# A graph layer with a residual and a layer norm on one core: runs of four rows for x, four unsplit chunks instead of six, ScalarE's normalise, and a new warm-up

## The chip, the cores and the metric

The kernel runs on one core of a Trainium2 chip. The metric is the device time of one execution in microseconds. The profile shows one execution, whose span is a little shorter than its device time.

## The reference

The inputs are x (4096 x 256, fp32) and an adjacency matrix adj (4096 x 4096, fp32, sparse, all entries at or above zero).

```python
mask = adj > 0
head = mask / max(sqrt(sum(mask * mask, axis=-1)), 1e-12)   # 1/sqrt(neighbours)
inc = adj + head
edge = (inc @ x) / sum(inc, axis=-1)
out = layernorm(x + edge, axis=-1)                          # eps 1e-5, no affine
```

The kernel works with inc scaled by the row's norm: the square root of the neighbour count times adj, plus the mask. The scale cancels between the product and the degree.

## The kernel before

**Layout.** A tile is 128 rows of adj; there are 32 tiles (`TILES`). A tile lies in SBUF as four quarters of [128 partitions x 1024]: quarter q holds rows 32q to 32q+31 of the tile, and partition block g (32 partitions) holds their columns 1024g to 1024g+1023. So a 32x32 block transpose of a quarter gives, for each of 32 chunks b, 128 values of the contraction dimension on the partitions. x is laid out the same way: partition 32g+j holds row 1024g+32b+j of x for chunk b.

**Per tile.** `sign_quarter` (L226, ScalarE) counts the positive entries of a quarter with an accumulated Sign. TensorE adds the partial sums of the four partition blocks with `quad_sum` (L650; in the warm-up L629, one matmul for each quarter). VectorE makes the count (`count_of` L453, `count_early` L447), GpSimd raises it to the power 0.5 (`norm_of` L360, `norm_early` L390). `scale_quarter` (L237, ScalarE) writes norm times adj to PSUM, `inc_quarter` (L465, VectorE) adds the mask, `transpose_quarter` (L481, VectorE) transposes into `incT`.

**The product.** fp32 matmuls run as two instructions for one chunk ("unsplit" or native, L655). To avoid them, 26 of the 32 chunks (`SPLIT`) are split in two parts of the type fp32r: `inc` into hi (rounded by ScalarE L248 for the quarters in `ACT_HI`, by GpSimd L385 for those in `POOL_HI`) and lo (the difference, GpSimd L380), x into hi (ScalarE L253) and lo (VectorE L441). A split chunk costs TensorE one matmul hi times (x hi, x lo) of 512 columns (L699) and one matmul lo times x hi of 256 columns (L708). The other six chunks (`NATIVE`) stay unsplit. Tiles 0 and 1 are unsplit altogether, for the split of x isn't there yet. Every tile accumulates in one of two PSUM tensors `edge`.

**The residual.** VectorE divides by the degree and adds x (L508, L512), takes statistics (L516, L521), GpSimd takes the power -0.5 (`rstd_of` L364), VectorE normalises (L533), SP stores.

**Order.** Every engine's instructions are written out by hand: VectorE works on tile t while TensorE is at tile t-1; `residual(t-2)` is threaded through VectorE's tile t and `normalise(t-3)` with it. ScalarE's `tile(t)` holds two scales of t, two signs of t+1, two signs of t+2, two scales of t+1 and two hi quarters of t. Raw tiles are double buffered: tile t+2's quarter k is loaded once `inc_quarter(t, k)` is done. SP issues all loads and stores in one queue; `store(t-4)` stands behind the loads of tile t. `sum_quadrants(t)` stands at position hi 3 of TensorE's tile t (`SUMS_AT`); it needs the signs of tile t+2, and `count_of(t+2)` on VectorE needs it. In the warm-up, tiles 0 to 3 (`EARLY`) have sums, counts and norms of their own for each quarter, so that a quarter can be scaled before the others have come.

## Time and profile before

| what | value |
|---|---|
| median of 3 runs | 427.29 us (424.83 to 427.61) |
| the profiled execution | 428.19 us, its span 426.4 us |
| busy share of the span | PE 93%, DVE 87%, ACT 81%, POOL 81% |
| chain that ended last | L699 35%, L708 18%, L655 15% (all PE) |
| mean granted clock of TensorE | 0.996 of full speed |
| HBM traffic | 79.7 MB, 187 GB/s over the span |

The chain is followed back from the last instruction. PE is the matmul engine, DVE is VectorE, ACT ScalarE, POOL GpSimd, SP the engine that issues DMAs. A mean duration counts from start to end, and two instructions that follow each other overlap a little; where that matters, start to start is read from a timeline.

### The profile page before, as it was taken

The page shows a single profiled execution, that of the slowest core. Times are in us where ns is not written, and L with a number is a line of the kernel's source. Part 1 is how long each engine was busy: PE and PEld are TensorE (multiplying, and loading weights), DVE is VectorE, ACT ScalarE, POOL GpSimd, SP SyncE. Part 2 cuts the span into 40 slices and gives each one's busy share as a digit, 9 for nine tenths or more (in the row PEclk, how much of TensorE's full clock was granted, in tenths as well). Part 3 has the DMA queues.
Part 4 walks back from the last instruction along what each step waited for, and adds up shares of the span by engine and source line. Part 5 has one row for each costly group of instructions (what it writes and reads, how often), then busy time and mean ns, then how long its engine had stood idle before and what let it go on. Part 6 is the DMA issues. An engine that isn't in the chain of part 4 may idle for free.

```text
span 426.4 us, 8925 instructions
## 1 busy us (share of the span) xinstructions
PE 396.4 (93%) x2174; PEld 349.5 (82%) x2174; DVE 370.9 (87%) x750; ACT 343.3 (81%) x450; POOL 344.2 (81%) x273
## 2 busy tenths in 40 slices
PE   1299987989999999999999999999999999999995
PEld 0277866868888888888888888888888888888884
DVE  0986776899999999999999999999999999999942
ACT  4874968989998888888989889898988988886300
POOL 3110386799999999999999999999999999999960
PEclk9999998999999999999999999999999999999999
DMA  8999986666766666666666666776666676670010
GB/s 231 258 233 244 261 220 182 173 190 200 215 188 197 194 203 216 213 196 192 200 184 200 186 200 202 221 212 190 200 186 199 186 199 194 206 221 25 26 38 12
DMA packets 38220, 79.86 MB, mean 187 GB/s; under 512 B 9536, under 2 KB 21824, under 8 KB 38208
## 3 DMA queue, kind: packets, MB, share of 16 engines
q1 hardware_dynamic: 37824, 78.68, 64.8%
q10 hardware_dynamic: 384, 1.05, 0.9%
q8 instruction: 4, 0.07, 0.1%
q14 instruction: 8, 0.07, 0.1%
HBM read 75.50 MB, written 4.19 MB: 187 GB/s over the span
## 4 chain that ended last, share of the span: by engine, by line
PE 70%; issue 3%; POOL 2%; DVE 2%; ACT 0%; POOLq 0%; DVEq 0%
PE edge L699 35%; PE edge L708 18%; PE edge L655 15%; POOL inc_split L380 2%; DVE inc L465 1%; PE sums L650 1%; DVE incT L481 1%; POOL inc_split L385 0%; ACT scaled L237 0%; POOLq L45 0%; POOL rstd L364 0%; DVE rows L533 0%; DVE rows L508 0%; DVE rows L512 0%; DVE stats L516 0%
## 5 line engine op out<-in xcount | busy, mean ns | idle before, releaser
L380 POOL TENSOR_TENSOR inc_split<-incT,inc_split 128x832 fp32r<-128x832 f32 x120 | 236.9, 1985 | 8.9 <-DVE incT L481 6.1
L699 PE MATMUL edge<-x_split,inc_split 128*128 128x512 f32 (+1 forms) x810 | 195.4, 392 | 0.0
L226 ACT ACTIVATE sign_out<-raw,sign_bias 128x1024 bf16<-128x1024 f32 x128 | 146.3, 1143 | 32.0 <-DMA raw<-in_adj_dram 30.5
L699 PEld LDWEIGHTS edge<-x_split,inc_split 128*128 128x128 f32 x810 | 145.9, 188 | 26.7
L465 DVE SCALAR_TENSOR_TENSOR inc<-raw,scaled 128x1024 f32<-128x1024 f32 x128 | 153.5, 1199 | 4.1 <-ACT scaled L237 4.1
L481 DVE STREAM_TRANSPOSE incT<-inc 128x1024 f32<-128x1024 f32 x128 | 155.8, 1227 | 0.2
L237 ACT ACTIVATE scaled<-raw,norm 128x1024 f32<-128x1024 f32 x128 | 141.7, 1107 | 13.2 <-POOL norm L390 6.6
L708 PEld LDWEIGHTS edge<-x_split,inc_split 128*128 128x128 f32 x780 | 99.1, 194 | 2.3
L708 PE MATMUL edge<-x_split,inc_split 128*128 128x256 f32 x780 | 100.0, 286 | 0.0
L655 PE MATMUL edge<-x_native,incT 128*128 128x256 f32 x384 | 92.2, 389 | 1.1 <-DVE count L447 0.7
L655 PEld LDWEIGHTS edge<-x_native,incT 128*128 128x128 f32 x384 | 71.9, 194 | 10.1 <-DVE incT L481 0.8
L248 ACT CAST inc_split<-incT 128x832 fp32r<-128x832 f32 x60 | 52.6, 876 | 9.8 <-DVE incT L481 8.0
L385 POOL TENSOR_SCALAR inc_split<-incT 128x832 fp32r<-128x832 f32 x60 | 55.1, 919 | 0.0
L390 POOL TENSOR_TENSOR norm<-count,half 128x1 f32<-128x1 f32 x16 | 8.9, 555 | 42.7 <-DVE count L447 42.7
L360 POOL TENSOR_TENSOR norm<-count,half 128x4 f32<-128x4 f32 x28 | 28.7, 1025 | 15.5 <-DVE count L453 15.5
L364 POOL TENSOR_TENSOR rstd<-var_eps,minus_half 128x1 f32<-128x1 f32 x32 | 17.9, 560 | 11.0 <-DVE var_eps L524 11.0
L655 PE MATMUL edge<-x_stage,incT 128*128 128x256 f32 x104 | 24.6, 386 | 0.8 <-DMA x_stage<-in_x_dram 0.8
L226 ACT ACTIVATION_READ_ACCUMULATOR sign_out<-raw,sign_bias 128x1 f32 x128 | 23.9, 187 | 0.0
L655 PEld LDWEIGHTS edge<-x_stage,incT 128*128 128x128 f32 x104 | 19.1, 190 | 4.3 <-DMA x_stage<-in_x_dram 2.0
L533 DVE TENSOR_SCALAR rows<-rows,mean_var,rstd 128x256 f32<-128x256 f32 x32 | 20.9, 655 | 1.6 <-POOL rstd L364 1.6
L508 DVE SCALAR_TENSOR_TENSOR rows<-edge,rdeg,rows 128x256 f32<-128x256 f32 x30 | 13.2, 439 | 10.2 <-PE edge L708 10.2
L453 DVE TENSOR_SCALAR count<-sums 128x4 f32<-128x4 f32 x28 | 4.5, 162 | 18.2 <-PE sums L650 18.2
(35 smaller groups left out, 119.5 us busy)
## 6 DMA issues: line engine op xcount, KB each, us to landing
raw<-in_adj_dram SPq DMA_DIRECT2D x504, 128.0 KB, 2.6
rows<-in_x_dram SPq DMA_DIRECT2D x32, 128.0 KB, 2.1
out_dram<-rows SPq DMA_DIRECT2D x32, 128.0 KB, 1.7
x_stage<-in_x_dram SPq DMA_DIRECT2D x8, 224.0 KB, 10.3
x_stage<-in_x_dram SPq DMA_DIRECT2D x8, 192.0 KB, 9.8
raw<-in_adj_dram ACTq DMA_DIRECT2D x8, 128.0 KB, 5.4
x_native<-in_x_dram SPq DMA_DIRECT2D x4, 192.0 KB, 7.3
```

Of the source, the lines that this page charges most:

```text
L226: nc.scalar.activation(sign_out[:, :], raw[:, s, q, :], ACT.Sign, scale=SIGN_SCALE, bias=sign_bias[:, 0:1], accum_out=part_sums[:, s, 1, q ...
L237: nc.scalar.mul(scaled[q % 2][:, :], raw[:, s, q, :], norm[:, s, q:q + 1]).then_inc(scaled_ready, 1)
L248: nc.scalar.copy(hi_of(s, q), incT[:, s, 0:SPLIT, q, :]).then_inc(hi_by_act, 1)
L360: nc.gpsimd.tensor_tensor(norm[:, s, :], count[:, s, :], half[:, :], ALU.pow).then_inc(norm_ready, 1)
L380: nc.gpsimd.tensor_tensor(lo_of(s, q), incT[:, s, 0:SPLIT, q, :], hi_of(s, q).bitcast(fp32), ALU.subtract).then_inc(lo_by_pool, 1)
L385: nc.gpsimd.tensor_scalar(hi_of(s, q), incT[:, s, 0:SPLIT, q, :], 1.0, 1.0, ALU.mult, ALU.mult).then_inc(hi_by_pool, 1)
L465: nc.vector.scalar_tensor_tensor(inc[:, q, :], raw[:, s, q, :], 0.0, scaled[q % 2][:, :], ALU.is_gt, ALU.add, accum_out=part_sums[:, s, 0, ...
L481: nc.vector.transpose(incT[:, s, :, q, :], inc[:, q, :].rearrange("p (b j) -> p b j", j=SQ)).then_inc(incT_ready, 1)
L533: nc.vector.tensor_scalar(result[:, s, :], y[:, s, :], mean_var[:, s, 0:1], rstd[:, s:s + 1], ALU.subtract, ALU.mult).then_inc(result_read ...
L655: return nc.tensor.matmul(edge[s][:, 0:D], incT[:, s, b, :, :].rearrange("p q j -> p (q j)"), x_of_b, start=start, stop=stop)
L699: last = nc.tensor.matmul(edge[s][:, c0:c1], inc_split[s][:, 0, b, :, :].rearrange("p q j -> p (q j)"), x_split[:, b, :, :].rearrange("p h ...
L708: last = nc.tensor.matmul(edge[s][:, D:2 * D], inc_split[s][:, 1, b, :, :].rearrange("p q j -> p (q j)"), x_split[:, b, 0, :], start=False ...
```

## The change

- x is laid out with four consecutive rows on one partition: partition 32g+j holds rows 128b'+4j+l of the block g for the chunks 4b'+l. A DMA run is then 4 KB (four rows) where it was 1 KB. To match, `transpose_quarter` reads inc with a stride of four elements (16 bytes) in place of unit stride.
- `NATIVE` goes from 6 to 4, so `SPLIT` from 26 to 28.
- ScalarE rounds three quarters of hi and GpSimd one (two and two before).
- The normalise moves from VectorE to ScalarE (Identity with scale rstd and bias shift); VectorE computes shift = -mean * rstd. The store stands one tile later in SP's queue.
- Sign writes int8 into two alternating buffers, with an immediate bias in place of one read from SBUF.
- `EARLY` goes from 4 to 6; the orders of the warm-up are rewritten on every engine, the last tiles are written out, and `SUMS_AT` goes from hi 3 to hi 12.

The core of the diff; ScalarE's, GpSimd's and VectorE's warm-up and tail are lists of calls in the same manner as the loops shown:

```diff
-    NATIVE = 6
+    NATIVE = 4
     SPLIT = B - NATIVE
     EPS = 1e-5
     SIGN_SCALE = 2.0 ** 60
     SIGN_BIAS = -2.0 ** -90
     FOUR_DMAS = 16 * G
+    EARLY = 6
     PORT_ORDER = [0, 2, 1, 3]
     adj_v = adj.rearrange("(t q r) (g c) -> t g r q c", q=G, r=SQ, g=G)
-    x_v = x.rearrange("(g b j) d -> g j b d", g=G, j=SQ)
+    x_v = x.rearrange("(g b j l) d -> g j b (l d)", g=G, j=SQ, l=4)
...
-        sign_out = sb("sign_out", [P, COLS], bf16)
+        sign_out = sb("sign_out", [P, 2, COLS], mybir.dt.int8)
...
+        shift = sb("shift", [P, 2], fp32)
...
+        early_sums = [[sums[0], sums[1], edge[0], edge[1]], [sums[0], sums[1], edge[1], sums[0]]]
+        early_sums += [[sums[1 - t % 2]] * G for t in range(2, EARLY)]
+        early_read = [[0, 0, 0, 0], [1, 2, 4, 5]] + [[8] + [G * t + q for q in range(1, G)] for t in range(2, EARLY)]
...
-        X_AT = [0, 7, 14, 20, SPLIT]
+        X_AT = [0, 8, 16, 24, SPLIT]
         X_PIECES = len(X_AT) - 1
-        EARLY = 4
-        ACT_HI = [0, 3]
-        POOL_HI = [1, 2]
+        ACT_HI = [0, 2, 3]
+        POOL_HI = [1]
...
+            def load_x(c):
+                for g in PORT_ORDER:
+                    sp.dma_start(x_stage[SQ * g:SQ * (g + 1), X_AT[c]:X_AT[c + 1], :].rearrange("p (b l) d -> p b (l d)", l=4),
+                                 x_v[g, :, X_AT[c] // 4:X_AT[c + 1] // 4, :]).then_inc(x_in[c], 16)
+            def load_x_native():
+                for g in PORT_ORDER:
+                    sp.dma_start(x_native[SQ * g:SQ * (g + 1), :, :].rearrange("p (b l) d -> p b (l d)", l=4),
+                                 x_v[g, :, SPLIT // 4:B // 4, :]).then_inc(x_native_in, 16)
             for k in range(G):
                 for g in (0, 1):
                     load_piece(sp, 0, 0, k, g)
-            for g in PORT_ORDER:
-                sp.dma_start(x_native[SQ * g:SQ * (g + 1), :, :], x_v[g, :, SPLIT:B, :]).then_inc(x_native_in, 16)
+            load_x_native()
             for k in range(G):
                 load_quarter(1, 1, k, False)
-            for c in range(4):
-                for g in PORT_ORDER:
-                    sp.dma_start(x_stage[SQ * g:SQ * (g + 1), X_AT[c]:X_AT[c + 1], :],
-                                 x_v[g, :, X_AT[c]:X_AT[c + 1], :]).then_inc(x_in[c], 16)
-            for s in range(2):
-                load_residual(s, s, False)
-            for s in range(2):
+            load_x(0)
+            load_x(1)
+            load_x(2)
+            load_x(3)
+            load_residual(0, 0, False)
+            for k in range(G):
+                load_quarter(2, 0, k, True)
+            load_residual(1, 1, False)
+            for k in range(G):
+                load_quarter(3, 1, k, True)
+            for t in range(4, 6):
                 for k in range(G):
-                    load_quarter(2 + s, s, k, True)
-            with sp.Fori(2, PAIRS) as u:
+                    load_quarter(t, t % 2, k, True)
+                if t == 5:
+                    store(0, 0)
+                load_residual(t - 2, t % 2, True)
+            with sp.Fori(3, PAIRS) as u:
...
-                    store(t - 4, s)
+                    store(t - 5, 1 - s)
...
-                    act.wait_ge(signs_ready, G * t + q)
+                    act.wait_ge(signs_ready, G * t + q - 1)
                 if early_reuse:
                     act.wait_ge(early_summed, G * (t - 2) + q + 1)
                 elif q == 0 and reuse:
                     act.wait_ge(summed, t - 3)
-                nc.scalar.activation(sign_out[:, :], raw[:, s, q, :], ACT.Sign, scale=SIGN_SCALE,
-                                     bias=sign_bias[:, 0:1], accum_out=part_sums[:, s, 1, q:q + 1]).then_inc(signs_ready, 1)
+                nc.scalar.activation(sign_out[:, q % 2, :], raw[:, s, q, :], ACT.Sign, scale=SIGN_SCALE,
+                                     bias=SIGN_BIAS, accum_out=part_sums[:, s, 1, q:q + 1]).then_inc(signs_ready, 1)
...
+            def normalise(t, s, u, reuse=True):
+                act.wait_ge(shift_ready, t + 1)
+                if reuse:
+                    act.wait_ge(stored[s], 16 * u)
+                nc.scalar.activation(result[:, s, :], y[:, s, :], ACT.Identity, scale=rstd[:, s:s + 1],
+                                     bias=shift[:, s:s + 1]).then_inc(result_ready, 1)
...
             sign_early(0, 0)
+            scale_early(0, 0)
             sign_early(0, 1)
-            scale_early(0, 0)
+            scale_early(0, 1)
             sign_early(0, 2)
-            scale_early(0, 1)
             sign_early(0, 3)
+            sign_early(1, 0)
             scale_early(0, 2)
             scale_early(0, 3)
-            sign_early(1, 0)
             sign_early(1, 1)
+            sign_early(1, 2)
             scale_early(1, 0)
-            sign_early(1, 2)
             scale_early(1, 1)
+            scale_early(1, 2)
             sign_early(1, 3)
-            scale_early(1, 2)
+            split_x_hi(0)
+            split_x_hi(1)
             scale_early(1, 3)
-            for c in range(X_PIECES):
-                split_x_hi(c)
+            split_x_hi(2)
+            split_x_hi(3)
...
+            with act.Fori(3, PAIRS - 2) as u:
+                scale_quarter(2 * u, 0, 2)
+                sign_quarter(2 * u + 1, 1, u, 2)
+                sign_quarter(2 * u + 1, 1, u, 3)
+                round_quarter(2 * u, 0, 0)
+                scale_quarter(2 * u, 0, 3)
+                normalise(2 * u - 3, 1, u - 2)
+                sign_quarter(2 * u + 2, 0, u + 1, 0)
+                scale_quarter(2 * u + 1, 1, 0)
+                sign_quarter(2 * u + 2, 0, u + 1, 1)
+                scale_quarter(2 * u + 1, 1, 1)
+                round_quarter(2 * u, 0, 2)
+                round_quarter(2 * u, 0, 3)
...
+            with pool.Fori(3, PAIRS - 2) as u:
+                norm_of(2 * u + 1, 1)
+                low_quarter(2 * u, 0, 0, behind=1)
+                round_quarter(2 * u, 0, 1, own=False)
+                rstd_of(2 * u - 2, 0)
+                low_quarter(2 * u, 0, 1)
+                low_quarter(2 * u, 0, 2)
+                low_quarter(2 * u, 0, 3)
...
-                nc.vector.transpose(incT[:, s, :, q, :],
-                                    inc[:, q, :].rearrange("p (b j) -> p b j", j=SQ)).then_inc(incT_ready, 1)
-            def residual(t, s, u, native=False):
-                def step(ins):
-                    ins.then_inc(dve_step, 1)
-                def after(k):
-                    dve.wait_ge(dve_step, steps_to(t) + k - (1 if native and k > 2 else 0))
+                nc.vector.transpose(incT[:, s, :, q, :].rearrange("p (b l) j -> p b l j", l=4),
+                                    inc[:, q, :].rearrange("p (b j l) -> p b l j", j=SQ, l=4)).then_inc(incT_ready, 1)
...
+            def shift_of(t, s):
                 dve.wait_ge(rstd_ready, t + 1)
+                nc.vector.scalar_tensor_tensor(shift[:, s:s + 1], mean_var[:, s, 0:1], -1.0, rstd[:, s:s + 1],
+                                               ALU.mult, ALU.mult).then_inc(shift_ready, 1)
...
+            with dve.Fori(3, PAIRS - 2) as u:
+                inc_quarter(2 * u, 0, 0)
+                degree(2 * u - 2, 0)
+                shift_of(2 * u - 3, 1)
+                inc_quarter(2 * u, 0, 1)
+                inverse_degree(2 * u - 2, 0)
+                transpose_quarter(2 * u, 0, 0)
+                y_first(2 * u - 2, 0, u - 1)
+                inc_quarter(2 * u, 0, 2)
+                y_second(2 * u - 2, 0)
+                count_of(2 * u + 1, 1)
+                transpose_quarter(2 * u, 0, 1)
+                statistics(2 * u - 2, 0)
+                inc_quarter(2 * u, 0, 3)
+                mean_variance(2 * u - 2, 0)
+                transpose_quarter(2 * u, 0, 2)
+                variance_eps(2 * u - 2, 0)
+                transpose_quarter(2 * u, 0, 3)
...
-                if t == 3 and q == 0:
-                    pe.wait_ge(dve_step, steps_to(0) + 1)
+                if t >= 3 and q == 0:
+                    pe.wait_ge(dve_step, steps_to(t - 3) + 1)
...
-            SUMS_AT = ("hi", 3)
...
+            sum_early(1, 2)
+            unsplit_chunks(0, 0, 0, B, {9: lambda: sum_early(1, 3), 18: lambda: sum_degree(0, 0)})
+            unsplit_chunks(1, 1, 0, B, {3: lambda: sum_early(2, 0), 7: lambda: sum_early(2, 1),
+                                        13: lambda: sum_early(2, 2), 16: lambda: sum_early(2, 3),
+                                        20: lambda: sum_degree(1, 1), 22: lambda: sum_early(3, 0),
+                                        31: lambda: sum_early(3, 1)})
+            tile(2, 0, {("native", 3): lambda: sum_early(3, 2), ("hi", 9): lambda: sum_early(3, 3),
+                        ("lo", 0): lambda: sum_early(4, 0), ("lo", 9): lambda: sum_degree(2, 0),
+                        ("lo", 10): lambda: sum_early(4, 1)}, first=True)
+            tile(3, 1, {("native", 2): lambda: sum_early(4, 2), ("hi", 8): lambda: sum_early(4, 3),
+                        ("hi", 10): lambda: sum_early(5, 0), ("hi", 18): lambda: sum_early(5, 1),
+                        ("hi", 22): lambda: sum_degree(3, 1)})
+            tile(4, 0, {("native", 0): lambda: sum_early(5, 2), ("native", 3): lambda: sum_early(5, 3),
+                        ("hi", 25): lambda: sum_quadrants(4, 0, early=True)})
+            tile(5, 1, {("hi", 18): lambda: sum_quadrants(5, 1, early=True)})
+            SUMS_AT = ("hi", 12)
+            with pe.Fori(3, PAIRS - 1) as u:
```

## Rows read from the trace of the kernel before

**Rows 1.** Chain that ended last, in order of time: start us, us, what.

```profile
207.55 2.59 PE edge L655 x12
210.14 0.71 PE edge L699 x4
...
210.97 5.33 PE edge L699 x23
216.30 3.11 PE edge L708 x26
219.42 2.59 PE edge L655 x12
```

**Rows 2.** Busy time of each engine in one tile: PE, PEld, DVE, ACT, POOL, clock, DMA.

```profile
210.14:222.01 11.87, 11.87 (x70) 10.56 (x69) 11.22 (x24) 10.63 (x15) 11.14 (x9) 1.00 0.65 195
```

**Rows 3.** Groups of instructions by form: busy us, mean ns, idle before, releaser.

```profile
L380 POOL TENSOR_TENSOR inc_split<-incT,inc_split 128x832 fp32r<-128x832 f32 x120 | 236.9, 1985 | 8.9 <-DVE incT L481 6.1 <-issue 0.2
...
L481 DVE STREAM_TRANSPOSE incT<-inc 128x1024 f32<-128x1024 f32 x128 | 155.8, 1227 | 0.2
...
L226 ACT ACTIVATE sign_out<-raw,sign_bias 128x1024 bf16<-128x1024 f32 x128 | 146.3, 1143 | 32.0 <-DMA raw<-in_adj_dram 30.5
...
L237 ACT ACTIVATE scaled<-raw,norm 128x1024 f32<-128x1024 f32 x128 | 141.7, 1107 | 13.2 <-POOL norm L390 6.6 <-DVE inc L465 3.6 <-POOL norm L360 2.4
...
L385 POOL TENSOR_SCALAR inc_split<-incT 128x832 fp32r<-128x832 f32 x60 | 55.1, 919 | 0.0
L248 ACT CAST inc_split<-incT 128x832 fp32r<-128x832 f32 x60 | 52.6, 876 | 9.8 <-DVE incT L481 8.0 <-PE edge L699 1.4
...
L533 DVE TENSOR_SCALAR rows<-rows,mean_var,rstd 128x256 f32<-128x256 f32 x32 | 20.9, 655 | 1.6 <-POOL rstd L364 1.6
...
L253 ACT CAST x_split<-x_stage 128x1792 fp32r<-128x1792 f32 x2 | 3.3, 1674 | 0.0
```

**Rows 4.** Timeline of ScalarE within one tile: start us, us, instruction.

```profile
212.80 1.10 ACT L237 ACTIVATE scaled<-raw,norm 128x1024 f32<-128x1024 f32 x1
213.84 1.13 ACT L226 ACTIVATE sign_out<-raw,sign_bias 128x1024 bf16<-128x1024 f32 x1
...
214.97 1.10 ACT L237 ACTIVATE scaled<-raw,norm 128x1024 f32<-128x1024 f32 x1
...
220.86 0.87 ACT L248 CAST inc_split<-incT 128x832 fp32r<-128x832 f32 x1
221.63 1.11 ACT L237 ACTIVATE scaled<-raw,norm 128x1024 f32<-128x1024 f32 x1
223.79 1.15 ACT L226 ACTIVATE sign_out<-raw,sign_bias 128x1024 bf16<-128x1024 f32 x1 [1.04 <-DMA raw<-in_adj_dram]
```

**Rows 5.** Timeline of VectorE: the count that waits for TensorE.

```profile
211.01 0.16 DVE L453 TENSOR_SCALAR count<-sums 128x4 f32<-128x4 f32 x1 [0.65 <-PE sums L650]
```

**Rows 6.** Timeline of TensorE in the first fifth of the span.

```profile
21.13 1.22 PE L655 MATMUL edge<-x_native,incT 128*128 128x256 f32 x2 [0.71 <-DVE count L447]
...
37.19 2.86 PE L655 MATMUL edge<-x_stage,incT 128*128 128x256 f32 x12 [0.66 <-DMA x_stage<-in_x_dram]
...
70.70 0.36 PE L650 MATMUL sums<-part_sums,quad_sum 128*128 128x8 f32 x2 [2.52 <-DVE incT L481]
...
100.56 2.75 PE L655 MATMUL edge<-x_native,incT 128*128 128x256 f32 x12
```

**Rows 7.** Timeline of ScalarE: the first sign of tile 2.

```profile
40.46 1.15 ACT L226 ACTIVATE sign_out<-raw,sign_bias 128x1024 bf16<-128x1024 f32 x1 [1.81 <-DMA raw<-in_adj_dram]
```

**Rows 8.** Three stretches of 2 us, columns as in Rows 2.

```profile
28.00:30.00 2.00, 2.00 (x11) 1.60 (x9) 1.97 (x4) 2.00 (x2) 0.00 (x0) 1.00 1.13 233
50.00:52.00 2.00, 2.00 (x12) 1.78 (x11) 1.41 (x3) 2.00 (x4) 1.17 (x2) 1.00 1.04 262
72.00:74.00 2.00, 2.00 (x11) 2.00 (x11) 0.35 (x1) 1.59 (x2) 2.00 (x3) 0.50 0.05 14
```

**Rows 9.** Timeline of VectorE: the last instruction of the last tile.

```profile
423.78 0.41 DVE L533 TENSOR_SCALAR rows<-rows,mean_var,rstd 128x256 f32<-128x256 f32 x1 [0.66 <-POOL rstd L364]
```

More of the change, by code:

```diff
@@ L314, in _ @@
             sign_early(3, 1)
+            normalise(0, 0, 0, reuse=False)
+            round_quarter(2, 0, 2, reuse=False)
             sign_early(3, 2)
@@ new lines, in _ @@
+            round_quarter(3, 1, 2, staged=True)
+            scale_early(4, 0)
+            round_quarter(3, 1, 3, staged=True)
+            sign_early(5, 0)
+            sign_early(5, 1)
+            scale_early(4, 1)
+            scale_early(4, 2)
+            normalise(1, 1, 0, reuse=False)
+            sign_early(5, 2)
+            sign_early(5, 3)
+            round_quarter(4, 0, 0)
+            scale_early(4, 3)
+            sign_early(6, 0)
+            scale_early(5, 0)
+            round_quarter(4, 0, 2)
@@ new lines, in _ @@
+            scale_quarter(28, 0, 2)
+            sign_quarter(29, 1, 14, 2)
+            sign_quarter(29, 1, 14, 3)
+            round_quarter(28, 0, 0)
+            scale_quarter(28, 0, 3)
+            normalise(25, 1, 12)
+            sign_quarter(30, 0, 15, 0)
+            scale_quarter(29, 1, 0)
+            sign_quarter(30, 0, 15, 1)
+            scale_quarter(29, 1, 1)
+            round_quarter(28, 0, 2)
+            round_quarter(28, 0, 3)
+            scale_quarter(29, 1, 2)
+            sign_quarter(30, 0, 15, 2)
@@ new lines, in _ @@
+            sign_quarter(30, 0, 15, 3)
+            round_quarter(29, 1, 0)
+            scale_quarter(29, 1, 3)
+            normalise(26, 0, 13)
+            sign_quarter(31, 1, 15, 0)
+            scale_quarter(30, 0, 0)
+            sign_quarter(31, 1, 15, 1)
+            scale_quarter(30, 0, 1)
+            round_quarter(29, 1, 2)
+            round_quarter(29, 1, 3)
+            scale_quarter(30, 0, 2)
+            sign_quarter(31, 1, 15, 2)
+            sign_quarter(31, 1, 15, 3)
+            round_quarter(30, 0, 0)
@@ new lines, in _ @@
+            scale_quarter(30, 0, 3)
+            normalise(27, 1, 13)
+            scale_quarter(31, 1, 0)
+            scale_quarter(31, 1, 1)
+            round_quarter(30, 0, 2)
+            round_quarter(30, 0, 3)
+            scale_quarter(31, 1, 2)
+            round_quarter(31, 1, 0)
+            scale_quarter(31, 1, 3)
+            normalise(28, 0, 14)
+            round_quarter(31, 1, 2)
+            round_quarter(31, 1, 3)
+            normalise(29, 1, 14)
+            normalise(30, 0, 15)
@@ L339, in _ @@
+            normalise(31, 1, 15)
         @block.gpsimd
@@ L391, in norm_early @@
                                         ALU.pow).then_inc(early_norm, 1)
-            def tile(t, s, more=True):
-                if more:
-                    norm_of(t + 1, 1 - s)
-                low_quarter(t, s, 0, True, behind=1)
-                round_quarter(t, s, 1)
-                rstd_of(t - 2, s)
-                low_quarter(t, s, 1, behind=2)
-                round_quarter(t, s, 2)
-                low_quarter(t, s, 2)
-                low_quarter(t, s, 3)
-            for t in range(3):
-                for q in range(G):
-                    norm_early(t, q)
@@ L431, in _ @@
-            tile(TILES - 2, 0)
-            tile(TILES - 1, 1, more=False)
-            for s in range(2):
-                rstd_of(TILES - 2 + s, s)
+            norm_early(5, 0)
+            rstd_of(2, 0)
+            low_quarter(4, 0, 0)
+            round_quarter(4, 0, 1)
+            norm_early(5, 1)
+            norm_early(5, 2)
+            low_quarter(4, 0, 1)
+            low_quarter(4, 0, 2)
+            norm_early(5, 3)
+            low_quarter(4, 0, 3)
+            round_quarter(5, 1, 1)
@@ L611, in _ @@
-            tile(TILES - 2, 0, PAIRS - 1)
-            tile(TILES - 1, 1, PAIRS - 1, more=False)
-            normalise(TILES - 3, 1, PAIRS - 2, True)
-            for s in range(2):
-                for _ in residual(TILES - 2 + s, s, PAIRS - 1):
-                    pass
-                normalise(TILES - 2 + s, s, PAIRS - 1, True)
+            transpose_quarter(1, 1, 1, slot_split=False, reuse_slot=False)
+            split_x_lo(0)
+            inc_quarter(1, 1, 2, reuse_deg=False)
+            split_x_lo(1)
```

540 lines of the change are left out of this document (360 added, 180 removed).

## Prediction

> **What bounds the kernel now.** I read the chain that ended last first. From about 92 us on it is TensorE alone, tile after tile, with the same four pieces and no gap: 2.59 for twelve unsplit matmuls, 0.71 and 5.33 for hi, 3.11 for lo, 0.12 for the sums, and the next tile begins 11.87 us after the last [rows 1]. The window over one tile says the same from the other side: PE busy 11.87 of 11.87, VectorE 11.22, GpSimd 11.14, ScalarE 10.63 [rows 2]. So in the steady part only TensorE's own work counts, as long as no other engine needs more than TensorE does. ScalarE's slack shows as a wait for a raw load (1.04, [rows 4]), VectorE's as the wait for the sums (0.65, [rows 5]): both are waits of engines that are early.
>
> The first part is different. TensorE begins the product at 21.13 and tile 5 at 100.56 [rows 6]. At full speed two unsplit tiles (27.7) and three split ones (35.6) would take 63.3, so 16.1 us are lost there, to x that comes late (0.66 and shorter waits, at 37.19), and to sums that wait (2.52 at 70.70) [rows 6]. Behind that wait the granted clock was 0.50 in 72 to 74 us, which is 1.2 GHz, after TensorE had stood still from 68.2 to 70.7 [rows 8].
>
> **The steady part of the change.** An unsplit chunk costs 2 x 2.59/12 = 0.432, a split one 5.33/23 + 3.11/26 = 0.232 + 0.120 = 0.351 [rows 1]. Two chunks a tile change sides: -0.16, so 11.70 a tile if TensorE stays the bound. For the 27 tiles 5 to 31 that is 4.35 us. Whether it stays the bound is arithmetic on three queues, start to start:
>
> ScalarE. A scale takes 1.04, a sign with its accumulator read 1.13, a cast 0.77 [rows 4]: 4.16 + 4.52 + 1.54 = 10.2 now. A cast grows by (1674 - 876)/960 = 0.83 ns an element [rows 3], so 64 more make 0.82, three of them 2.47. A cast of 1024 would be 1036 ns by that slope where the sign is 1143; the sign reads its bias from SBUF, the cast nothing. So a sign without that read is 1.03, four 4.1. The normalise of 256 elements: 876 - 576 x 0.83 = 400, and two operands read from SBUF at 0.1 each, 0.6 long and 0.5 start to start. Sum 4.1 + 4.16 + 2.47 + 0.5 = 11.2, with 0.5 left under 11.70. If the sign stays at 1.13 it is 11.6. The Trainium skill, "ScalarE: Activation LUTs", section "What ACT_TABLE_LOAD costs", gives 93 ns for each pointer operand; the rows' 107 agree, and with 93 the sum would be 11.3. The alternating sign buffer takes away a wait of some 0.1 between two signs in a row, and the load that ScalarE waits for now stands behind a store that waits for the normalise; the store moves a tile later, so SP isn't held by it. I count these at nothing: they refill slack that the sum uses up.
>
> GpSimd. One round less, -0.92; four lows of 896 in place of 832, 4 x 1.985 x 64/832 = +0.61 and +0.07 for the round that stays [rows 3]: 11.14 - 0.24 = 10.9.
>
> VectorE. The normalise goes (0.65 [rows 3], some 0.6 start to start) and a one-column instruction comes (0.1): 11.22 becomes 10.7, plus whatever the stride costs in four transposes. 1.0 is left under 11.70: **0.25 for each transpose is free, all above it is paid 4 times a tile.** No row shows a read with a stride of 16 bytes. From below the bound is 0: nothing of the pattern can make the read shorter than the one in order. From above I take a second pass over the 1024 elements, at the slope of the casts 0.85, at worst 1.05. I take 0, for the nearest row is the transpose itself: 1227 ns for 1024 elements [rows 3], one plain pass with one operand read, although its output already jumps after every 32 elements. Against it speaks a rule. The Trainium skill, "SBUF — State Buffer", in its note on SBUF cachelines, says that each access to a new 16-byte line pays a penalty and that two hits on a line are needed for full speed, yet names four fp32 elements as a free stride in the same note; every access here goes to a new line. By its strict reading the transposes stretch (the third case below), by its loose one they don't; no run here shows which.
>
> The order. The sums move from hi 3 to hi 12, to 1.73 + 12 x 0.232 + 0.12 = 4.6 after a tile's start. VectorE has then to do the count, three transposes, one inc and small steps, 5.3, so its last transpose ends near 10.1 of 11.7; the last hi quarter is cast by ScalarE at about 11.2, and needed at 11.7 + 1.73. ScalarE's two signs that the sums need are done near 2.8 of the tile, before 4.6 (and would be late for hi 3 at 2.4: the move has a reason). GpSimd's fourth low ends near 4.3 of the next tile, lo begins at 8.3. Every wait on this way has over a microsecond in hand, so TensorE has no gap.
>
> **The warm-up.** Behind x everything is bound by the transfers: the DMA engines are full (share over 1.0) both at 28 us, where x comes in runs of 1 KB at 233 GB/s, and at 50 us, where adj comes in runs of 4 KB at 262 [rows 8]. x is 4.19 MB, 18.0 us against 16.0: all behind it comes 2.0 us sooner, with the second residual after tile 2 another 0.4. Step by step:
> Tile 0: its last transpose now stands behind the count of sign (1, 1), and I work out a start at 22.7, 1.5 later than 21.13 [rows 6]. That is hidden: the last piece of x lands near 35.3 (37.19 less 1.9), four chunks (1.73) are left after it, and by its own work tile 0 ends at 22.7 + 13.8 + 0.4 = 36.9. Tile 1 starts at 37.2.
> Tile 1: 13.8 of product, seven sums of 0.12. The first sign of tile 2 was at 40.46 behind a load [rows 7], now 38.1; its sum stands at chunk 3 (38.6) and waits 0.7, the fourth one, loads 2 us apart, about 0.5. Tile 2 starts at 53.2, and VectorE has its last transpose at 52.7.
> Tiles 2 to 4: 11.7 each, with five, four and three early sums (some 0.5 a tile) and up to 0.5 for hi quarters or sums that come just in time. I get 65.9, 78.7 and 90.9 for the starts of tiles 3, 4 and 5. No wait over 1 us is left in this walk, so no drop of the clock either. Against 100.56 [rows 6] that is 9.7 us. The bounds: all steps on time, and PE alone from 37.2, gives 37.2 + 14.7 + 3 x 12.1 = 88.2, 12.4; half of the gain lost to steps that miss by a microsecond, 95.7, 4.9.
>
> **The tail.** After the last product VectorE's 0.41 [rows 9] is replaced by the shift (0.15), a hop (0.2) and ScalarE's 0.6: +0.5.
>
> **Sum.** -4.35 - 9.7 + 0.5 = -13.55. Against the profiled 428.19 this is 414.6, against the median, 0.9 lower, 413.7. I say 414.
>
> **Rivals.**
> 1. ScalarE becomes the bound. Its 11.2 to 11.6 leaves 0.1 to 0.5, and it has waits on VectorE of 0.2 now. For it: a third cast waits for the last transpose of a tile. Against it: those waits lie where it is early. At 11.9 a tile in place of 11.70 it costs 27 x 0.2 = 5.4: 419 to 420. By the same size the half-lost warm-up gives 418.5.
> 2. The start isn't won: if the walk of tiles 0 to 4 misses as now, only -4.35 + 0.5 remains, 423.5. For it: 16 us are lost now in steps that the walk prices at 6, and ScalarE and VectorE run nearly full there. Against it: two causes of the loss, the runs of 1 KB and the sums of a whole tile for tile 4, are gone.
> 3. The other side: the strided transposes are slow. With D more for each, VectorE needs 10.7 + 4D a tile, and it decides from D = 0.25 on. With D = 0.6 (half of a second pass) 13.1 a tile, 27 x 1.4 = 38 over the forecast, 452; with D = 1.05 a tile is 14.9, 27 x 3.2 = 86, with 10 more in the warm-up, 510. For it: nothing in the trace excludes it. Against it: the jumps of its output cost nothing that shows in its 1227 ns. In the mild case (D below 0.25) only the warm-up feels it, by 1 to 2.
>
> **Chances.** Forecast, within 410 to 418: 0.60. Rival 1 or half the warm-up, 418 to 421.5: 0.17. Rival 2: 0.06. Rival 3: 0.14. Better than 410: 0.03. The range that leaves out no more than 2 in 10 reaches from 409.5 to 424, past rivals 1 and 2, short of rival 3. One per cent, 4.3 us, is about what a measurement can tell: faster (below 423) 0.82, within 0.04, slower 0.14.
>
> **What would show it.** L481's mean first of all: 1227 right, above 1480 rival 3. Then the tile in the chain: 11.70, with 1.73 for unsplit; ScalarE below 11.4 a tile and no wait of PE for a cast (rival 1); a sign at 1.04 and not 1.14; windows at 28 us with 260 GB/s; the start of tile 5 near 91; PEclk without a drop near 72. I'd be wrong above all by a stride that costs, then by early steps that meet late.

## The result and the profile after

The changed kernel takes 532.21 us (median of 4 runs, 531.63 to 534.89), the kernel before 427.45 beside it: 1.246 times as long (95% interval 1.240 to 1.252). I had said 414, so the forecast is wrong in its sign. The profiled execution took 531.63 with a span of 529.8.

The head of the page of the changed kernel, and its section on the chain that ended last:

```profile
span 529.8 us, 8912 instructions
...
PE 424.4 (80%) x2190; PEld 365.3 (69%) x2190; DVE 498.0 (94%) x756; ACT 378.0 (71%) x512; POOL 336.8 (64%) x248
...
issue 45%; DVE 44%; PE 4%; DVEq 2%; ACT 2%; POOL 2%; ACTq 1%; POOLq 0%
```

VectorE is busy 94% of the span and TensorE has 4% of the chain, where it had all of it in the steady part before [rows 1]. The "issue" entries of the chain lie inside VectorE's long instructions (the profile shows no releaser there). VectorE itself has hardly a gap: from 110.51 to 510.56 us, the starts of tiles 5 and 31 on TensorE, it is busy 399.42 of 400.05. One tile of the changed kernel, columns as in [rows 2]:

```profile
249.06:264.43 15.37, 12.00 (x67) 10.38 (x67) 15.37 (x25) 11.72 (x16) 10.78 (x8) 1.00 0.52 154
```

15.37 of 15.37 on VectorE, against 11.87 a tile before [rows 2]. From the start of tile 5 to the end of the last product it is 413.7 us where it was 320.6, which is 93.1 of the 103.4 by which the span grew (27 times 3.50 would be 94.5). Tile 5 begins at 110.51 and not at 100.56 [rows 6], which is another 10.0. The groups by form of the changed kernel, in the order of their busy time:

```profile
L629 DVE STREAM_TRANSPOSE incT<-inc 128x1024 f32<-128x1024 f32 x128 | 257.3, 2023 | 0.3
...
L613 DVE SCALAR_TENSOR_TENSOR inc<-raw,scaled 128x1024 f32<-128x1024 f32 x128 | 153.9, 1203 | 0.0
...
L234 ACT ACTIVATE sign_out<-raw 128x1024 int8<-128x1024 f32 x128 | 133.4, 1042 | 0.0
...
L256 ACT CAST inc_split<-incT 128x896 fp32r<-128x896 f32 x90 | 84.6, 940 | 105.6 <-DVE incT L629 105.5
...
L685 DVE SCALAR_TENSOR_TENSOR shift<-mean_var,rstd 128x1 f32<-128x1 f32 x32 | 49.5, 1548 | 0.7 <-POOL rstd L452 0.7
...
L268 ACT ACTIVATE rows<-rows,shift,rstd 128x256 f32<-128x256 f32 x32 | 18.8, 588 | 14.8 <-DVE shift L685 14.8
```

Two groups are out of line. The transpose takes 2023 ns where it took 1227 [rows 3]. And the shift, one column wide, takes 1548 ns; I had put 0.1 us for it. The other groups are as priced.

What the shift does in its 1.5 us is seen by laying two timelines of the changed kernel side by side. VectorE, at the start of the tile above:

```profile
250.25 1.72 DVE L685 SCALAR_TENSOR_TENSOR shift<-mean_var,rstd 128x1 f32<-128x1 f32 x1
251.90 1.21 DVE L613 SCALAR_TENSOR_TENSOR inc<-raw,scaled 128x1024 f32<-128x1024 f32 x1
```

GpSimd at the same time:

```profile
247.80 6.24 POOL L468 TENSOR_TENSOR inc_split<-incT,inc_split 128x896 fp32r<-128x896 f32 x3
```

Three subtractions of 2.08 us follow each other, so the second ends at 251.96. The shift, begun at 250.25, ends at 251.97: it ends with the GpSimd instruction that was in flight. Its shortest case in this trace is 155 ns, its median 1728. And it is a rule of this trace: 29 of the 32 shifts begin while a subtraction is under way, and all 29 end 0.01 to 0.02 after it. The other three begin with GpSimd idle and take 0.16.

### The profile page after: what moved, and what is told of

It reads as the page before. It is cut to its first block, busy times and chain, and to the rows that moved or that the text cites. A ratio compares the mean times of both kernels' runs of the same rounds, so it can differ in the third digit from the quotient of the medians.

```text
span 529.8 us, 8912 instructions
## 1 busy us (share of the span) xinstructions
PE 424.4 (80%) x2190; PEld 365.3 (69%) x2190; DVE 498.0 (94%) x756; ACT 378.0 (71%) x512; POOL 336.8 (64%) x248
## 4 chain that ended last, share of the span: by engine, by line
issue 45%; DVE 44%; PE 4%; DVEq 2%; ACT 2%; POOL 2%; ACTq 1%; POOLq 0%
DVE inc L613 22%; DVE incT L629 11%; PE edge L951 3%; DVE rows L661 2%; DVE stats L671 2%; DVE rows L666 2%; DVE shift L685 1%; POOL inc_split L468 1%; PE edge L996 1%; ACT sign_out L234 1%; DVE x_split L589 1%; ACTq L153 1%; DVE var_eps L680 1%; DVEq L612 1%; DVE mean_var L676 1%
## 5 line engine op out<-in xcount | busy, mean ns | idle before, releaser
L468 POOL TENSOR_TENSOR inc_split<-incT,inc_split 128x896 fp32r<-128x896 f32 x120 | 251.0, 2114 | 24.9 <-DVE incT L629 22.5
L629 DVE STREAM_TRANSPOSE incT<-inc 128x1024 f32<-128x1024 f32 x128 | 257.3, 2023 | 0.3
L996 PE MATMUL edge<-x_split,inc_split 128*128 128x512 f32 (+1 forms) x870 | 218.7, 404 | 0.0
L996 PEld LDWEIGHTS edge<-x_split,inc_split 128*128 128x128 f32 x870 | 164.3, 198 | 32.1
L256 ACT CAST inc_split<-incT 128x896 fp32r<-128x896 f32 x90 | 84.6, 940 | 105.6 <-DVE incT L629 105.5
L234 ACT ACTIVATE sign_out<-raw 128x1024 int8<-128x1024 f32 x128 | 133.4, 1042 | 0.0
L1005 PEld LDWEIGHTS edge<-x_split,inc_split 128*128 128x128 f32 x840 | 104.8, 191 | 2.3
L685 DVE SCALAR_TENSOR_TENSOR shift<-mean_var,rstd 128x1 f32<-128x1 f32 x32 | 49.5, 1548 | 0.7 <-POOL rstd L452 0.7
L482 POOL TENSOR_SCALAR inc_split<-incT 128x896 fp32r<-128x896 f32 x30 | 28.3, 944 | 2.8 <-DVE incT L629 2.8
L268 ACT ACTIVATE rows<-rows,shift,rstd 128x256 f32<-128x256 f32 x32 | 18.8, 588 | 14.8 <-DVE shift L685 14.8
L234 ACT ACTIVATION_READ_ACCUMULATOR sign_out<-raw 128x1 f32 x128 | 23.9, 187 | 0.0
```

What stands on the lines that cost most here:

```text
L234: nc.scalar.activation(sign_out[:, q % 2, :], raw[:, s, q, :], ACT.Sign, scale=SIGN_SCALE, bias=SIGN_BIAS, accum_out=part_sums[:, s, 1, q: ...
L256: nc.scalar.copy(hi_of(s, q), incT[:, s, 0:SPLIT, q, :]).then_inc(hi_by_act, 1)
L468: nc.gpsimd.tensor_tensor(lo_of(s, q), incT[:, s, 0:SPLIT, q, :], hi_of(s, q).bitcast(fp32), ALU.subtract).then_inc(lo_by_pool, 1)
L482: nc.gpsimd.tensor_scalar(hi_of(s, q), incT[:, s, 0:SPLIT, q, :], 1.0, 1.0, ALU.mult, ALU.mult).then_inc(hi_by_pool, 1)
L629: nc.vector.transpose(incT[:, s, :, q, :].rearrange("p (b l) j -> p b l j", l=4), inc[:, q, :].rearrange("p (b j l) -> p b l j", j=SQ, l=4 ...
L685: nc.vector.scalar_tensor_tensor(shift[:, s:s + 1], mean_var[:, s, 0:1], -1.0, rstd[:, s:s + 1], ALU.mult, ALU.mult).then_inc(shift_ready, 1)
```

## The experiments

**e1: the disputed costs by themselves.** A small program with the instructions alone. The transposes and the inc-like instruction are written once for each access pattern; then a shift in two forms and the transposes run beside a row of GpSimd's subtractions. The forms of the transpose and of the shift:

```
transpose(low in order, inc.rearrange("p (b j l) -> p b l j", j=32, l=1, 2, 4 or 8))
scalar_tensor_tensor(shift, mean, -1.0, rstd, mult, mult)     # two operands of SBUF
tensor_scalar(shift, mean, rstd, -1.0, mult, mult)            # one, and rstd as its scalar
```

> The disputed prices by themselves, nothing of the reference is computed. Theory: the stride of 16 bytes costs the transpose 0.8 us with no other engine at work (about 2.0 against 1.2 for 1024 elements), and the one-column instruction with two SBUF operands takes 0.1 to 0.2 us alone, but up to 2.1 beside GpSimd's subtractions, for it waits until the one in flight ends; the form with one SBUF operand and a pointer scalar stays at 0.1 to 0.2. Rival on the stride: the slow transposes come from sharing SBUF with GpSimd, then stride 4 alone takes 1.2. Where the price begins is open: stride 2 (8 bytes) and stride 8 (32 bytes) tell. Rival on the shift: it is slow by itself, then it takes 1.5 alone too.

Groups by form of the probe:

```profile
L95 DVE STREAM_TRANSPOSE low<-inc 128x1024 f32<-128x1024 f32 x6 | 12.0, 2006 | 0.2
L93 DVE STREAM_TRANSPOSE low<-inc 128x1024 f32<-128x1024 f32 x6 | 11.9, 1982 | 0.2
L99 DVE SCALAR_TENSOR_TENSOR low<-raw,scaled 128x1024 f32<-128x1024 f32 x6 | 11.7, 1958 | 0.2
L104 DVE SCALAR_TENSOR_TENSOR low<-raw,scaled 128x1024 f32<-128x1024 f32 x6 | 11.7, 1957 | 0.2
L114 DVE STREAM_TRANSPOSE low<-inc 128x1024 f32<-128x1024 f32 x4 | 8.1, 2013 | 0.1
L70 ACT ACTIVATE scaled<-raw 128x1024 f32<-128x1024 f32 x4 | 7.9, 1964 | 0.1
L89 DVE STREAM_TRANSPOSE low<-inc 128x1024 f32<-128x1024 f32 x6 | 7.5, 1246 | 20.5 <-ACT rstd L74 20.4
L91 DVE STREAM_TRANSPOSE low<-inc 128x1024 f32<-128x1024 f32 x6 | 7.5, 1246 | 0.2
L97 DVE SCALAR_TENSOR_TENSOR low<-raw,scaled 128x1024 f32<-128x1024 f32 x6 | 7.3, 1221 | 0.2
...
L68 ACT ACTIVATE scaled<-raw 128x1024 f32<-128x1024 f32 x4 | 4.1, 1027 | 0.1
L111 DVE SCALAR_TENSOR_TENSOR shift<-mean,rstd 128x1 f32<-128x1 f32 x4 | 3.5, 862 | 0.1
...
L112 DVE TENSOR_SCALAR shift<-mean,rstd 128x1 f32<-128x1 f32 x4 | 0.9, 214 | 0.1
```

L89, L91, L93 and L95 read with strides of 1, 2, 4 and 8 elements: 1246, 1246, 1982, 2006 ns. It is a step between 8 and 16 bytes and not a slope; from 16 bytes to 32 it hardly grows. It isn't the transpose's own either: the two-operand instruction goes from 1221 (L97) to 1958 with a strided read (L99) and to 1957 with a strided write alone (L104), and ScalarE from 1027 (L68) to 1964 (L70) with a strided read. The difference on 1024 elements is 0.74 to 0.76 us on VectorE, six tenths of the instruction's time again, and 0.94 on ScalarE, nine tenths of it. The transpose is hardly slower beside GpSimd (L114, 2013), so GpSimd is not what makes it 2023 in the changed kernel. The two-operand shift has 862 in the mean in the part beside GpSimd and 159 alone; the one-operand form 214 both ways. The 862 is no price either: two of the four took 0.15 and 0.16 (one began before GpSimd did, one at the very start of a subtraction), the other two 1.47 and 1.67. Both theories of the expectation came.

One of the two long shifts of L111, all engines of the probe:

```profile
95.72 5.22 POOL L121 TENSOR_TENSOR half<-raw 128x896 f32<-128x896 f32 x3
...
99.48 1.47 DVE L111 SCALAR_TENSOR_TENSOR shift<-mean,rstd 128x1 f32<-128x1 f32 x1
```

95.72 + 5.22 = 100.94 is the end of the third subtraction, 99.48 + 1.47 = 100.95 that of the shift.

**e2: the kernel before, with the stride alone.**

```diff
-                nc.vector.transpose(incT[:, s, :, q, :],
-                                    inc[:, q, :].rearrange("p (b j) -> p b j", j=SQ)).then_inc(incT_ready, 1)
+                nc.vector.transpose(incT[:, s, :, q, :].rearrange("p (b l) j -> p b l j", l=4),
+                                    inc[:, q, :].rearrange("p (b j l) -> p b l j", j=SQ, l=4)).then_inc(incT_ready, 1)
```

> The kernel before with strided reads in the transposes and nothing else; x stays in its old layout, so the product pairs rows of x wrongly. Theory: each transpose 2.0 us, VectorE 11.2 + 3.2 = 14.4 a tile, it becomes the bound, 27 x 2.6 = 70 and some 8 more in the warm-up: 505 us. Rival (the stride is slow only together with the rest of the change): 427 to 435 us.

498.53 us, 1.167 (1.164 to 1.169). A stretch of it, which is a little longer than a tile:

```profile
200.00:214.42 14.42, 12.41 (x69) 10.58 (x68) 14.42 (x24) 10.99 (x15) 11.10 (x8) 1.00 0.58 172
```

VectorE never stands still: from tile 5's start (109.32) to tile 31's (478.81) it is busy 369.49 of 369.49 us. That is 14.2 a tile; by VectorE's 11.22 of before [rows 2] and four times 0.80 it would be 14.4. Of the 0.2 between them 0.1 is the normalise, which takes 546 ns in the mean here and took 655 before [rows 3]. This one edit, of two lines, costs 71 us: 61 of them lie behind tile 5's start, 9 in the warm-up. The 505 of the expectation was 6 too high, as it took 14.4 for the tile.

**e3: the changed kernel without the stride.** The diff of e2 the other way round, in the changed kernel.

> The changed kernel with transposes that read in order; x stays in the new layout, so rows of x are paired wrongly. Theory: VectorE falls from 15.37 to 12.2 a tile and is still the bound through the shift, which stays near 1.5 us; 27 x 3.2 = 86 and some 10 in the warm-up come back: 436 us, above the kernel before. Rival (the wait of the shift is an accident of the phase and goes with the stride): 11.7 a tile, 415 to 420 us.

419.05 us, 0.980 (0.978 to 0.982). The rival in its expectation was right. One tile of e3:

```profile
218.88:230.58 11.70, 11.70 (x69) 10.40 (x68) 11.38 (x24) 11.60 (x17) 10.79 (x8) 1.00 0.65 201
```

The shift's group by form in e3:

```profile
L685 DVE SCALAR_TENSOR_TENSOR shift<-mean_var,rstd 128x1 f32<-128x1 f32 x32 | 27.8, 868 | 0.7 <-POOL rstd L452 0.7
```

TensorE is the bound again, at the 11.70 of the prediction. The shift still waits, 0.87 in the mean, yet VectorE has room for it: in most tiles it begins 1.34 into a subtraction and has 0.8 left to wait.

One case is out of line. The traced execution took 425.39 us, and in it stand, on VectorE, GpSimd and TensorE:

```profile
95.24 5.51 DVE L685 SCALAR_TENSOR_TENSOR shift<-mean_var,rstd 128x1 f32<-128x1 f32 x1
...
94.46 6.27 POOL L468 TENSOR_TENSOR inc_split<-incT,inc_split 128x896 fp32r<-128x896 f32 x3
...
110.28 3.78 PE L951 MATMUL edge<-x_native,incT 128*128 128x256 f32 x8 [4.22 <-DVE incT L629]
```

This shift begins during the first of three subtractions in a row and ends, at 100.75, with the third (94.46 + 6.27 = 100.73). It let two go by where the others waited for one at most. The transposes behind it come late, TensorE stands still for 4.22 and then has a granted clock of 0.50 (1.2 GHz) up to 113.50, and two tiles take 16.08 and 14.73. Two of the six executions of e3 took 424.14 and 425.39, the other four 418.01 to 419.38; of the 42 of e4 and of e6 to e12, which have the other form of the shift, none took more than 419.58. So in e3 the wait is worth nothing in most executions, and 7 us in this one. Whether the 424.14 had the same cause was not traced.

**e4: e3 with the shift in the form of one operand.**

```diff
-                nc.vector.scalar_tensor_tensor(shift[:, s:s + 1], mean_var[:, s, 0:1], -1.0, rstd[:, s:s + 1],
-                                               ALU.mult, ALU.mult).then_inc(shift_ready, 1)
+                nc.vector.tensor_scalar(shift[:, s:s + 1], mean_var[:, s, 0:1], rstd[:, s:s + 1], -1.0,
+                                        ALU.mult, ALU.mult).then_inc(shift_ready, 1)
```

> As e3, and the shift made by an instruction with one SBUF operand and a pointer scalar, which should not wait for GpSimd. Theory, and the walk of the prediction: VectorE 10.7 a tile, TensorE the bound at 11.70, tile 5 at 91 us, 414 us. Rivals: ScalarE bounds at 11.9 (420 us); the warm-up is not won (423 us); the shift still waits (as e3).

418.49 us, 0.979 (0.976 to 0.981), no different from e3's median. One tile of e4:

```profile
212.42:224.12 11.70, 11.70 (x69) 10.40 (x68) 10.78 (x24) 11.53 (x17) 10.78 (x8) 1.00 0.66 200
```

The shift's group by form in e4:

```profile
L685 DVE TENSOR_SCALAR shift<-mean_var,rstd 128x1 f32<-128x1 f32 x32 | 6.6, 207 | 0.7 <-POOL rstd L452 0.7
```

VectorE falls from 11.38 to 10.78 and the tile doesn't move.

**e5: the changed kernel, stride and all, with e4's shift.**

> The changed kernel, strides kept, with the shift made from one SBUF operand and a pointer scalar. Theory: in the changed kernel the shift waits 1.5 us a tile for a subtraction of GpSimd, and VectorE is the bound, so all of it is paid: 15.37 - 1.5 = 13.85 a tile, 27 x 1.5 = 41 and a few more in the warm-up, 488 us. Rival (as in e3, where the same edit was worth nothing: the time moves into another wait): 525 to 532 us.

493.09 us, 1.153 (1.150 to 1.156), where I had expected 488. One tile of it:

```profile
248.86:262.75 13.89, 12.05 (x67) 10.38 (x67) 13.89 (x24) 11.72 (x16) 10.77 (x8) 1.00 0.56 169
```

The tiles are not all alike here: most lie between 13.8 and 14.3, and 14.04 is their mean. So the same edit that is worth nothing in e3's median is worth 532.2 - 493.1 = 39.1 us here. From tile 5's start to the last product's end it takes 376.9 us, the changed kernel 413.7: 36.8 of the 39.1 lie there, the rest in the warm-up. VectorE is the bound, and all that it waits is paid. With e4 it splits the loss: stride alone leads from e4's 418.5 to 493.1 (74.6), the shift from there to 532.2 (39.1).

**e6, e7, e8: what the runs of x are worth.** e6 is e4 with x in runs of one row (1 KB), which needs no rearrangement at all; e7 with runs of two rows (2 KB) and a stride of two elements, which e1 had shown to be free; e8 is e7 with a first piece of four chunks in place of eight.

```diff
-    x_v = x.rearrange("(g b j l) d -> g j b (l d)", g=G, j=SQ, l=4)
+    x_v = x.rearrange("(g b j l) d -> g j b (l d)", g=G, j=SQ, l=1)
```

(and l=1 in the loads and the transposes; l=2 throughout in e7 and e8.) In e8 also:

```diff
-        X_AT = [0, 8, 16, 24, SPLIT]
+        X_AT = [0, 4, 12, 20, SPLIT]
```

> All of the change but the stride: x in its old layout in runs of 1 KB, transposes in order, the shift from one SBUF operand. Theory: the runs of 4 KB were worth little, for tile 0 is released by the first piece of x and not by the last; 1 to 2 us above e4's 418.5: 420 us. Rival (the transfers set the whole warm-up): 421.5 or more.

> As e6 with runs of two rows (2 KB) and transposes with a stride of two elements (8 bytes), which took 1.25 us alone in e1. Theory: transposes stay at 1.23 in the kernel too, 418.5 to 419.5 us. Rival (stride 2 costs once GpSimd and the DMA write beside it): transposes above 1.4, VectorE over 11.6 a tile, 425 us or more.

> As e7 with pieces of x of 4, 8, 8 and 8 chunks, so that the first one is half as large. Theory: in e4 tile 0's product began at 23.8 and then waited for the first piece until 27.4; with half the piece 1 to 2 us of that go: 417 us. Rival (tile 1 then waits for its transposes, or for its own early sums): as e7.

418.73 (0.979, 0.977 to 0.981), 418.79 (0.979, 0.976 to 0.981) and 418.9 (0.979, 0.977 to 0.981): with e4's 418.49 four versions that can't be told apart. The rival of e7 (a stride of two elements costs beside the other engines) didn't come: its transposes take 1231 ns. Nor did the gain that I expected of e8. In 28 to 30 us they moved 231 (e6), 239 (e7) and 240 GB/s (e4), but that is no clean effect of the runs: the changed kernel, e3 and e5, with runs of 4 KB too, have 244, 231 and 234, and e2 with runs of 1 KB has 246. The last piece of x lands at 36.6 in e6, at 35.4 in e7 and at 35.2 in e4, so longer runs may bring it some 1 us sooner, and nothing waits for it. TensorE's timeline of e8, the start of tile 0, shows what it is doing instead:

```profile
23.79 3.78 PE L951 MATMUL edge<-x_native,incT 128*128 128x256 f32 x8 [2.43 <-DVE incT L629]
27.37 3.55 PE L951 MATMUL edge<-x_stage,incT 128*128 128x256 f32 x10
```

Eight records in 3.58 us start to start, 0.43 each but for the first; from 31 us on they follow at 0.22. It waits for no transfer: it works at half its rate, after it had nearly stood still for the first 23 us.

**e9, e10, e11: the start of tile 0.** e9 is e6 with products of constants, written to columns that nobody reads, on TensorE while it would stand still. e10 is e6 with two steps of tile 1 earlier. e11 is both. In e9 and e11:

```diff
+            def keep_warm(n):
+                pe.wait_ge(early_count, 3)
+                for _ in range(n):
+                    nc.tensor.matmul(edge[0][:, 256:384], quad_sum[:, :], quad_sum[:, :], start=True, stop=True)
...
             sum_early(1, 0)
+            keep_warm(7)
             sum_early(1, 1)
             sum_early(1, 2)
+            keep_warm(10)
```

In e10 and e11:

```diff
+            count_early(1, 2)
             inc_quarter(1, 1, 0, reuse_deg=False)
             inc_quarter(1, 1, 1, reuse_deg=False)
-            count_early(1, 2)
...
-            unsplit_chunks(0, 0, 0, B, {9: lambda: sum_early(1, 3), 18: lambda: sum_degree(0, 0)})
+            unsplit_chunks(0, 0, 0, B, {5: lambda: sum_early(1, 3), 18: lambda: sum_degree(0, 0)})
```

> As e6, with 17 matmuls of 128 columns on constants (their result is never read) in TensorE's idle time before tile 0, 7 between the sums (1, 0) and (1, 1) and 10 before the product. Theory: the first chunks of tile 0 ran at half rate (two matmuls of 0.43 us for a chunk where 0.22 is the rule) because TensorE had stood idle; with work before them they run at full rate, tile 0 takes 14.2 instead of 16.2 to 17.2, and 1 to 2.5 us are won before VectorE's transposes of tile 1 hold it: 417 us. Rival (the first chunks wait for x, not for a clock): nothing, 418.7 us.

> As e6, with VectorE's count (1, 2) ahead of two incs and the sum (1, 3) at chunk 5 of tile 0 instead of 9; no extra matmuls. Theory: ScalarE's wait of 3 us for norm (1, 2) goes, the last transpose of tile 1 comes 2 us sooner, but tile 0 ends at 40 as before: 0.2 us, 418.5 us. Rival (the transposes of tile 1 are what counts): 417 us.

> e9 and e10 together. Theory: tile 0 ends about 2.5 us sooner and finds tile 1's transposes ready, so all of it counts unless the loads of tile 2 take over: 416 us. Rival (the loads of tile 2 set its start whatever tile 1 does): as e6, 418.7 us.

417.99 (0.978, 0.975 to 0.980), 417.15 (0.976, 0.973 to 0.978) and 417.23 (0.976, 0.973 to 0.978). TensorE's timeline of e10, without the products of constants:

```profile
23.79 3.78 PE L951 MATMUL edge<-x_native,incT 128*128 128x256 f32 x8 [2.15 <-DVE incT L629]
```

And of e11, with them:

```profile
23.79 1.99 PE L951 MATMUL edge<-x_native,incT 128*128 128x256 f32 x8 [0.30 <-DVE incT L629]
...
35.02 5.45 PE L951 MATMUL edge<-x_stage,incT 128*128 128x256 f32 x24 [0.57 <-DMA x_stage<-in_x_dram]
```

Kept at work, TensorE does the same eight records in 1.99 in place of 3.78, so the half rate does come from its standing still. But now it is early and waits: 0.70 for a sign of tile 1 and 0.57 for the third piece of x. Tile 1 begins at 40.30 where e10 has 40.68, and the time is no shorter than e10's.

In e9 the constants cost what they save. TensorE's timeline of e9:

```profile
21.21 4.32 PE L1017 MATMUL edge<-quad_sum 128*128 128x128 f32 x20
25.37 1.89 PE L951 MATMUL edge<-x_native,incT 128*128 128x256 f32 x8
```

The second row of them runs slowly itself (4.32 here, 2.48 in e11) and holds the product until 25.37 where it could begin at 23.79. Tile 1 begins at 40.02, in the trace of e6 at 40.01, and the two traced executions took 418.02 and 418.05; the 0.7 between the medians is not explained by them. e10 is 1.6 us shorter than e6 by the two earlier steps of tile 1 alone, as the rival in its expectation had it, and in e11 the constants add nothing to that.

**e12: e11 with runs of two rows.** Now that x is waited for, its runs should count.

> e11 with x in runs of two rows and transposes with a stride of two elements. Theory: in e11 TensorE waited 0.6 us for a piece of x at 35.0, so the transfers of x are now what holds tile 0; runs of 2 KB move 5 to 10 GB/s more than runs of 1 KB, all behind them comes up to 1 us sooner: 416.5 us. Rival (longer runs are worth nothing, as between e6 and e7): 417.2 us.

416.66 us, 0.974 (0.972 to 0.977), the shortest of all. TensorE waits for no piece of x now (for a sign of tile 1 still 1.04), and tile 1 begins at 39.46, 0.8 before e11's. From e11 it is 0.6, which this measurement can't tell from nothing; from the kernel before it is 2.6%.

## Why the prediction was wrong

**The step that failed: "I take 0".** This is where VectorE's four transposes are priced. Their stride costs 0.80 each, 3.2 a tile. My reason was that the nearest row is the transpose itself, whose output already jumps after every 32 elements. That row was near in name only: its output jumps once in 32 elements, the new read at every one. The second pass that I had as a bound from above (0.85) was nearly the right size. The rule of the Trainium skill, "SBUF — State Buffer", in the note on SBUF cachelines, holds in its strict reading (two hits on a 16-byte line are needed): 8-byte steps are free and 16-byte steps are not, in e1. Its loose reading, four fp32 elements for free, is refuted by L93. I gave the two readings no weight of their own, and put 0.14 on the case that happened.

**The term that was missing: the shift at 0.1.** It took 1.55, which turned rival 3's "10.7 + 4D" into "12.2 + 4D". That formula was otherwise right: with D = 0.80 it gives 13.9, and e5 shows 13.89 in the tile above and 14.04 in the mean; the shift's wait makes it 15.37. At D = 0.80 the rival by itself gives 414 + 27 x 2.2 and up to 10 for the warm-up, 473 to 483. The run with the stride alone took 493.1 (e5): its tile 5 begins at 108.26, 17 behind the 90.9 of the walk and not 10. The rival's worst case of 510 is still 22 short of the 532 that came. The signal was in [rows 3]: the normalise on VectorE, which the change replaced, had a mean of 655 there for 256 columns, and the same instruction at [rows 9], with GpSimd idle, took 0.41. I read 0.65 as its price. Over the whole trace it was 411 at the least, 622 in the median and 1758 at the most. One of the long cases, in VectorE's timeline of the kernel before:

```profile
405.19 1.76 DVE L533 TENSOR_SCALAR rows<-rows,mean_var,rstd 128x256 f32<-128x256 f32 x1
```

And GpSimd's timeline of the kernel before, at the same time:

```profile
404.81 1.98 POOL L380 TENSOR_TENSOR inc_split<-incT,inc_split 128x832 fp32r<-128x832 f32 x1
```

The one ends at 406.95, the other at 406.79. So it is in every tile: 30 of the 32 begin while a GpSimd instruction is under way, and each of them ends 0.15 after it; the two with GpSimd idle take 0.41. The 0.65 in the mean were 0.4 of work and some wait for GpSimd, and that wait doesn't shrink with the columns, as the 0.4 does. The Trainium skill, "GPSIMD Engine Reference", section "Key points", names contention of GpSimd with VectorE instructions that have two SBUF inputs (the shift) or run in a two-port mode; the traces agree for the shift, and the size is the rest of GpSimd's instruction, up to 1.9 here, or two more instructions on top of it in the one case of e3. Which of its two cases the normalise of 256 columns falls under, no run here shows.

**The steady part otherwise held.** Without the stride a tile takes the 11.70 of the forecast (e3, e4), GpSimd 10.78 (said 10.9), VectorE 10.78 (said 10.7), ScalarE 11.53 (said 11.2, or 11.6 at worst). The prices of ScalarE's instructions were right: the cast is 932 to 940 ns and the normalise 588, as priced, the sign 1042 in place of 1143, just the 0.1 of the operand that it no longer reads. What the 11.2 lacks was there before: the sum began from 10.2 where [rows 2] had 10.63. So rival 1 didn't come: 11.53 is under 11.70. The sums at hi 12 make TensorE wait nowhere in the steady part.

**The warm-up.** With the stride gone tile 5 begins at 94.73 (e4), a gain of 5.8 against the 9.7 of the walk and just over its lower bound of 4.9. The whole miss is in tile 0: from start to start the walk has 53.7 from tile 1 to tile 5, e4 53.8. Tile 0 was to begin at 22.7 and take until 37.2; it began at 23.78 and took until 40.93. Of these 3.7 us 1.1 is the later start. Some 2.5 are the half rate, for the walk let TensorE work at full rate from the first matmul: the first eleven in e4 took 4.9 us, start to start, and would have taken 2.4. [rows 6] had this: two records in 1.22. The walk also had x as the limit there. Its last piece landed at 35.2 (35.3 in the walk), though at 240 GB/s and not at 262, and TensorE, slower than thought, waited for none of it. The granted clock doesn't show the half rate (1.00 in e4's stretch of 23.80 to 27.40), so it has to be read from the distance of the matmuls.

**The tail.** From the last product's end to the last instruction's end it was 3.04 before and 3.48 in e4: +0.44 where +0.5 was said.

**The sum without the stride.** From tile 5's start to the last product's end e4 takes 316.8 where it was 320.6: -3.8, for one tile takes 12.12 and every second one 11.73. With -5.8 and +0.4 that is -9.2, by which the span of e4 is shorter. The forecast of 414.0 with the 3.8 of tile 0 is 417.8, and with the 0.6 of the tiles (-3.8 in place of -4.35) 418.4; e4 has 418.49. It lies in the range of 409.5 to 424 and beside the figure that rival 1 had for a half-lost warm-up, but by tile 0's rate, which no rival named.

## What to carry to other kernels

Look at the innermost step of every operand, reads and writes: where it is 16 bytes or more, price 0.7 to 0.9 us more for 1024 elements, on VectorE and on ScalarE, before asking what the layout wins. Read the least, median and greatest duration of VectorE's small instructions beside a busy GpSimd: where they spread, the mean is a wait and not a price, and for a one-column instruction a form with one SBUF operand and a scalar took it away. A wait costs nothing until its engine is the bound, so two costs on one engine aren't judged one by one: the shift was worth 0 in e3's median and 39 us in e5. Even off the bound a wait is a risk: in one execution of e3 it grew to 5.5 us and cost 7.
